# Perceiver block on one core: the context of the cross-attention is loaded in both layouts, and its layer norm moves into weights and probabilities

## What is computed

```python
    def _L0_xattn_ref(modality1, modality2, ln1_g, ln1_b, ln2_g, ln2_b, Wq, bq, Wk, bk, Wv, bv, Wo, bo):
        ...
        E = Wq.shape[1]
        scaling = E ** (-0.5)
        x1 = layernorm(modality1, ln1_g, ln1_b)
        x2 = layernorm(modality2, ln2_g, ln2_b)
        q = x1 @ Wq + bq
        k = x2 @ Wk + bk
        v = x2 @ Wv + bv
        scores = jnp.einsum('bqe,bke->bqk', q, k) * scaling
        attn = jax.nn.softmax(scores, axis=-1)
        ctx = jnp.einsum('bqk,bke->bqe', attn, v)
        return ctx @ Wo + bo
    ...
    x = x + _L0_xattn_ref(_layernorm(x, axis=-1), ctx_768, ...)
```

## Time and profile before

| | |
|---|---|
| median of 3 runs | 584.26 us (583.65 to 586.27) |
| the profiled execution, its own time | 584.41 us |
| its span | 582.5 us |
| TensorE busy | 504.2 us, 87% |
| VectorE busy | 390.8 us, 67% |
| ScalarE busy | 284.8 us, 49% |
| GpSimd busy | 115.6 us, 20% |
| moved by DMA | 98.74 MB, mean 170 GB/s |

### The profile page before, as it was taken

How to read it: one execution, slowest core, us unless ns; L and a number is a source line. 1 busy time by engine, 2 the same in 40 slices (tenths; PEclk the granted TensorE clock), 3 DMA queues, 4 the chain that set the end, 5 groups by cost and what they waited for, 6 DMA issues and landing times.

```text
span 582.5 us, 11091 instructions
## 1 busy us (share of the span) xinstructions
PE 504.2 (87%) x3601; PEld 294.1 (50%) x3602; DVE 390.8 (67%) x876; ACT 284.8 (49%) x449; POOL 115.6 (20%) x89
## 2 busy tenths in 40 slices
PE   5799999989989899976720699999999999999993
PEld 3674656474657577755420244444444444544441
DVE  2889779827987989889785666665563736673230
ACT  0662768685356666666610444463544525552130
POOL 1212113112323040400670002112111111121112
PEclk9899999999989999996755789999999999999998
DMA  9992606000006996162397358987584875744232
GB/s 323 390 383 101 218 1 217 2 1 2 1 0 249 379 382 239 38 217 77 128 307 252 55 179 254 258 262 221 126 244 117 231 218 159 235 80 87 54 54 37
DMA packets 54962, 98.74 MB, mean 170 GB/s; under 512 B 25073, under 2 KB 26257, under 8 KB 50833
## 3 DMA queue, kind: packets, MB, share of 16 engines
q1 hardware_dynamic: 23984, 74.81, 36.7%
q10 hardware_dynamic: 26640, 13.73, 9.8%
q0 software_dynamic: 4304, 9.77, 7.8%
HBM read 63.36 MB, written 29.43 MB: 159 GB/s over the span
## 4 chain that ended last, share of the span: by engine, by line
PE 69%; DVE 11%; ACT 6%; issue 5%; POOL 5%; DMA 3%; SPq 0%; ACTq 0%; POOLq 0%; DVEq 0%
PE bank L695 20%; PE bank L713 19%; PE bank L343 7%; PE bank L511 5%; POOL routed_rows L1637 3%; PE bank L495 2%; PE bank L425 2%; PE bank L455 2%; PE bank L361 2%; PE bank L405 2%; PE bank L537 2%; PE bank L476 1%; DMA routed_rows<-shared,ints 1%; ACT ctxT_region L741 1%; PE bank L588 1%
## 5 line engine op out<-in xcount | busy, mean ns | idle before, releaser
L695 PE MATMUL bank<-wbuf,ctx_region 128*128 x504 | 116.2, 388 | 6.3 <-issue 5.3
L1419 DVE SCALAR_TENSOR_TENSOR wbuf<-ctx_region,wbuf 128x2048 f32 (+1 forms) x28 | 62.9, 2289 | 31.9 <-ACT wbuf L880 31.9
L1667 POOL DMA_INDIRECT out<-misc,ints x21 | 38.6, 1839 | 229.7 <-ACT misc L961 174.5
L695 PEld LDWEIGHTS bank<-wbuf,ctx_region 128*128 128x128 f16 x504 | 49.0, 100 | 65.7 <-issue 13.5
L880 ACT ACTIVATE wbuf<-ctx_region 128x2048 f32 (+1 forms) x28 | 51.9, 1902 | 28.7 <-issue 22.5
L1569 POOL TENSOR_TENSOR small<-small 128x2 f32<-128x2 f32 (+2 forms) x25 | 29.5, 1182 | 173.8 <-DVE small L1034 167.2
L713 PE MATMUL bank<-wbuf,actT 128*128 x264 | 58.8, 379 | 1.0 <-DVE actT L1529 1.0
L980 ACT ACTIVATE ctxT_region<-bank 128x512 f32<-128x512 f32 x42 | 25.1, 597 | 67.9 <-PE bank L695 67.9
L713 PE MATMUL bank<-wbuf,xn 128*128 x240 | 53.4, 379 | 0.0
L511 PE MATMUL bank<-ctx_region,wbuf 128*128 128x256 f16 x384 | 44.9, 279 | 4.3 <-DVE ctx_region L1165 3.4
L511 PEld LDWEIGHTS bank<-ctx_region,wbuf 128*128 128x128 f16 x384 | 38.1, 100 | 11.2 <-DVE ctx_region L1165 4.1
(11 more groups left out here) (214 smaller groups left out, 820.0 us busy)
## 6 DMA issues: line engine op xcount, KB each, us to landing
ctx_region<-in_experts SPq DMA_DIRECT2D x28, 1024.0 KB
routed_rows<-ctxT_region SPq DMA_DIRECT2D x1, 16900.0 KB, 50.7
ctx_region<-in_ctx SPq DMA_DIRECT2D x8, 1536.0 KB, 8.9
ctx_region<-routed_rows ACTq DMA_DIRECT2D x23, 260.0 KB, 3.6
wbuf<-in_experts SPq DMA_DIRECT2D x4, 1024.0 KB
out<-x ACTq DMA_DIRECT2D x8, 256.0 KB
x<-in_x SPq DMA_DIRECT2D x1, 1536.0 KB, 14.3
wbuf<-in_wqT SPq DMA_DIRECT2D x4, 256.0 KB, 4.1
```

Of the source, the lines that this page charges most:

```text
L695: mm = nc.tensor.matmul(bank[half][:, :], xgT[:, b, x_part, k * P:(k + 1) * P], w16[:, ds(at + (w_part + k * EH + half * 512), 512)], star ...
L1419: nc.vector.scalar_tensor_tensor(w16[:, ds(at + (LOW + n * PIECE), PIECE)], src_[:, piece], W_SCALE, w16[:, ds(at + (HIGH + n * PIECE), PI ...
L1667: nc.gpsimd.indirect_dma_start(out, bass.IndirectOffsetOnAxis(idx[:, slot_no:slot_no + 1].bitcast(U32), axis=0), y_out[:, slot_no, :], Non ...
```

## The change

The context is no longer normalised. It is read raw, in two layouts: `ctx_768` as before from SyncE's queue, and a new input `ctxT`, the same numbers already turned on the host (left key included), 1.58 MB a tile, from ScalarE's queue straight into `ctxT_region`. The mean is taken out of the weights (`fold` subtracts from Wk's rows, already times the norm's gain, their mean over the channels; the sums over the context get their own mean subtracted by ScalarE), gain and shift of the norm go into Wk, the bias terms and `m2`. The inverse root of each key multiplies the scores and, after the softmax, the probabilities:

- TensorE: `context_T` and the turning of the left keys go; `roots_spread` comes, once a pair, with 16 products of 32x128 and 8 of 32x1 that lay each key's inverse root along a row for all 128 queries.
- ScalarE: `ctx_copies` and `ctx_norm` go; `load_ctxT` (two issues a pair, each behind the scores that free its slot), `roots_out` (2 copies of 257 columns), `queries_scaled` (2 of 128x512, before on VectorE), a sum, a small step and a second pass on each `cv` come; the copies of `pT` and `p_left` go to VectorE.
- VectorE: `ctx_scale`, `left_keys` and half of `sums_low` go; the scores' product with the spread roots, `probs_scaled`, `fold` and `value_bias` come; `ctx_stats` stays in full, and moves behind `probs_scaled`.
- SyncE: context tiles 6 and 7 are now followed by the self-attention's weights, which were early before.

```diff
             sp.dma_start(x_tiles[:, 0:2], x_dram[:, 0:2]).then_inc(s["x_in0"], 16)
+            sp.dma_start(ln2_rows, t_in["ln2_rows"]).then_inc(s["ln2_in"], 16)
...
-            for tile in range(4, TILES):
-                sp.wait_ge(s["cv_ps"], tile - 3)
-                load_ctx(tile)
+            for pair in range(1, PAIRS):
+                if pair + 1 < PAIRS:
+                    for t in range(2):
+                        sp.wait_ge(s["cv_ps"], 2 * pair - 1 + t)
+                        load_ctx(2 * pair + 2 + t)
+                if pair == 2:
+                    sp.wait_ge(s["qkb_ps"], 1)
+                    load_w(swq, "swqT", s["self_qk_in"])
+                    load_w(swk, "swkT", s["self_qk_in"])
+            load_w(swv, "swvT", s["self_vo_in"])
+            load_w(swo, "swoT", s["self_vo_in"])
...
             for e in range(KC):
-                if e % 2 == 0:
-                    pe.wait_ge(qk_in[e // 2], 64)
+                pe.wait_ge(qk_in[e], 32)
+                pe.wait_ge(s["folded"], e + 1)
...
+            def roots_spread(pair):
+
+                pe.wait_ge(s["x1T"], pair + 1)
+                pe.wait_ge(s["cx_rstd"], 2 * pair + 2)
+                if pair == 0:
+                    pe.wait_ge(s["left_rstd"], 1)
+                for t in range(2):
+                    tile = 2 * pair + t
+                    for b in range(BT):
+                        rows_of, at = slice(b * L, (b + 1) * L), dict(start=True, stop=True, tile_position=(0, b * L), skip_group_check=True)
+                        for c2 in range(2):
+                            nc.tensor.matmul(bank[t][rows_of, c2 * P:(c2 + 1) * P],
+                                             cx_rstd[:, tile % 4, 2 * b + c2:2 * b + c2 + 1].to_broadcast([P, L]), ident, **at)
+                        mm = nc.tensor.matmul(bank[t][rows_of, KEYS - 1:KEYS],
+                                              ident[0:B, tile * BT + b:tile * BT + b + 1].to_broadcast([B, L]), l_rstd[0:B, :], **at)
+                    mm.then_inc(s["r_ps"], 1)
...
                 for k in range(CC):
                     if k == 1:
                         pe.wait_ge(s["q_bias"], 1)
+                        roots_spread(0)
+                    if k == 2:
+                        pe.wait_ge(s["r_out"], 2)
...
-                    context_T(2 * pair + 2)
                     asked(pair + 1)
-                    context_T(2 * pair + 3)
+                    roots_spread(pair + 1)
                     sums_T(pair)
...
+            def load_ctxT(tile):
+                act.dma_start(ctxT[:, tile % 2].rearrange("p c b k -> p (c b k)"), t_in["ctxT"][tile]).then_inc(ctxT_in[tile % 2], 16)
...
+            queries_scaled(1)
+            roots_out(0)
             for pair in range(PAIRS):
...
+                    nc.scalar.activation(cv[:, t, :], bank[2 + t][:, 0:DC], ACT.Copy, scale=sc_rinv[:, t:t + 1],
+                                         accum_out=cv_sum[:, t:t + 1]).then_inc(s["cv_raw"], 1)
+                    act.wait_ge(s["cv_raw"], 2 * tile + 1)
+                    nc.scalar.activation(cv_shift[:, t:t + 1], cv_sum[:, t:t + 1], ACT.Copy, scale=-1.0 / DC).then_inc(s["cv_raw"], 1)
+                for t in range(2):
+                    act.wait_ge(s["cv_raw"], 4 * pair + 2 * t + 2)
+                    scaled(cv[:, t, :], cv[:, t, :], 1.0, cv_shift[:, t:t + 1]).then_inc(s["cv"], 1)
...
+            def fold(e):
+
+                dve.wait_ge(qk_in[e], 32)
+                key_w = wkT[:, e, 0:DC]
+                count(nc.vector.scalar_tensor_tensor(unread[:, 0:DC + 1], wkT[:, e, 0:DC + 1], 1.0, ln2_b_row[:, 0:DC + 1], ALU.mult,
+                                                     ALU.mult, accum_out=wkT[:, e, DC:DC + 1]), "norm_step")
+                count(nc.vector.scalar_tensor_tensor(key_w, key_w, 1.0, ln2_g_row, ALU.mult, ALU.mult,
+                                                     accum_out=wk_sum[:, e:e + 1]), "norm_step")
+                nc.vector.scalar_tensor_tensor(key_w, wk_sum[:, e:e + 1].to_broadcast([P, DC]), -1.0 / DC, key_w, ALU.mult,
+                                               ALU.add).then_inc(s["folded"], 1)
...
-                    count(nc.vector.tensor_reduce(sc_max[:, one], bank[2 + t][:, 0:KEYS], AX.X, ALU.max), "max_step")
+                    count(nc.vector.tensor_tensor(of_keys, bank[2 + t][:, 0:KEYS], spread[:, t, 0:KEYS], ALU.mult), "max_step")
+                    count(nc.vector.tensor_reduce(sc_max[:, one], of_keys, AX.X, ALU.max), "max_step")
...
+            def probs_scaled(pair):
+                for t in range(2):
...
+                    nc.vector.tensor_tensor(pT[:, t, :].rearrange("p (c b q) -> p c b q", c=2, b=BT),
+                                            bank[4 + t][:, 0:2 * P].rearrange("p (c b q) -> p c b q", c=2, b=BT),
+                                            cx_rstd[:, tile % 4, :].rearrange("p (b c) -> p c b", c=2)[:, :, :, None].to_broadcast(by_key),
+                                            ALU.mult).then_inc(s["pT"], 1)
```

More of the change, by code:

```diff
@@ L610, in logits @@
                     mm.then_inc(s["z_ps"], 1)
-            context_T(0)
-            pe.wait_ge(s["left_n"], 1)
-            transposes(bank[7][:, 320:416], [left_n[0:B, k * P:(k + 1) * P] for k in range(CC)], s["left_ps"])
             asked(0)
-            context_T(1)
             for pair in range(PAIRS):
@@ L851, in _ @@
+                    nc.scalar.copy(x2a[:, 0, :, t * P:(t + 1) * P], bank[4 + t][:, 0:DC].rearrange("p (k t) -> p k t", k=CC))\
+                        .then_inc(s["x2a_hi"], 1)
+                if pair + 2 < PAIRS:
+                    queries_scaled(pair + 2)
             cut_self_high(2)
@@ L1053, in ctx_stats @@
-            def ctx_stats(tile):
-                u, part = tile % 2, ctx_n[:, tile % 4]
-                if tile == 2 or tile % 2 and tile > 1:
-                    dve.wait_ge(s["cx_n1"], halved(tile - 2))
-                dve.wait_ge(ctx_in[tile % 4], 16 * (tile // 4 + 1))
-                pieces = [part[:, b, c2, :] for b in range(BT) for c2 in range(2)]
-                norm_stats(pieces, cx_stats[:, u], cx_mv[:, u], cx_ve[:, u], s["cx_ve"])
-            def ctx_scale(tile):
+            def ctx_stats(tile, parts=(0, 1)):
@@ L1071, in ctx_scale @@
-                for i, piece in enumerate(pieces[0:4] if half else pieces):
-                    op = normalise(piece, piece, cx_mv[:, u, i, 0:1], cx_rstd[:, u, i:i + 1])
-                op.then_inc(s["cx_n0"], 1)
+                if 0 in parts:
+                    if tile > 1:
+                        dve.wait_ge(s["cx_rstd"], tile - 1)
+                    dve.wait_ge(ctx_in[tile % 4], 16 * (tile // 4 + 1))
+                    for i in range(4):
+                        count(nc.vector.bn_stats(cx_stats[:, u, i, :], pieces[i]), "norm_step", wait=False)
@@ L1098, in queries_low @@
                 nc.vector.tensor_tensor(x1[:, 1], x1T, x1[:, 0], ALU.subtract).then_inc(s["x1_lo"], 1)
-            def left_keys(pair):
-                for t in range(2):
-                    tile = 2 * pair + t
-                    nc.vector.tensor_copy(ctxT[:, t, :, :, KEYS - 1], left_T[:, :, tile * BT:(tile + 1) * BT]).then_inc(s["left_cols"], 1)
             def context_max(pair):
```

336 lines of the change are left out of this document (158 added, 178 removed).

## The result

The changed kernel takes 590.28 us (median of 6 runs, 586.6 to 592.77) against 584.17 in the runs beside it: ratio 1.0099, 95% interval 1.0058 to 1.014. It is slower by about 6 us, where 4.7 us less were predicted. The profiled execution takes 591.1 us with a span of 588.8 (before 584.41 and 582.5). Executions of one kernel differ (the mean granted clock of the six of the change lies between 0.925 and 0.934), so a trace stands for one execution, and its time is given where it lies far from the median.

What follows compares the result with a forecast made beforehand. TensorE was taken as the bound (busy 87% of the span, 26.2 us a pair). Pairs -9.1, head +3.0 and tail +1.4 sum to -4.7, so 584.4 becomes 579.7 us (579.6 against the median); range 571 to 590.

Steps and rivals of the forecast that it cites:

- Removal of the turning: TensorE's context transposes and the waits on their copies go: 7.38 us a pair, 22.1 us in three pairs.
- The spread: New root products on TensorE, once a pair: 4.2 us taken, with ends of 1.5 and 6.9.
- the dear rival: Spread on TensorE at 6.9 us a pair, kernel slower than before at 590 us; chance 0.16.
- The head: Up to the first sums: scores 11 us early, but first sums at 62.3 instead of 59.31, 3.0 us more.
- The clock in the pairs: Three pairs: no term for lower clock, 2.5 us added only before the first sums; below 1.0 would contradict the prediction.
- The tail: After the last sums, extra passes on each cv: 1.4 us more before the self-attention.
- Behind the stage: After about 145 us no instruction changes; everything there is taken to move as a whole.
- VectorE's 21.2 us a pair: VectorE's work in a pair sums to 21.2 us, below TensorE's 23.0, with 1.8 us to spare.
- the transfers at nothing: Later context tiles and ctxT's issues on ScalarE are taken to cost no time; as a rival 586 us, chance 0.10.
- the prediction's own signs of being wrong: First sums after 66, clock below 1.0 in pairs, scores waiting for DMA, or a difference behind the self-attention's start.
- Rival (b): Spread dear: 6.9 us a pair, pairs 1.2 less, head 5.5 more, tail 1.4: +5.7, 590 us; chance 0.16.
- Rival (a): Spread cheap: four column tiles overlap, 1.5 us a pair, VectorE becomes the bound: 572.7 us; chance 0.20.

Runs made afterwards that it cites:

- e7_left_last: Changed kernel with the spread's one-column products moved behind the wide ones, whose order stays: 574.85 us, ratio 0.9822 to the kernel before.
- e2_wide_left: Changed kernel with the spread's order kept and its one-column products run over 128 rows: 580.12 us, ratio 0.9904 to the kernel before.
- e5_no_turned_loads: Changed kernel with turned context loaded only for tiles 0 and 1, later pairs' scores reading those: 588.86 us, ratio 1.0079 to the kernel before.
- e1_order: Changed kernel with the spread's loops exchanged (neighbours on different column tiles) and one-column products behind the wide ones: 574.74 us, ratio 0.9805 to the kernel before.
- e8_all: Changed kernel with loops exchanged, one-column products last on 128 rows, second join ahead of first spread, VectorE reordered in first pair: 573.23 us, ratio 0.9808.
- e12_last_wide: Changed kernel with one-column products last and on 128 rows, wide ones in the change's order: 574.52 us in a single execution.
- e6_no_spread: Changed kernel without a spread in pairs 1 to 3, which use the first pair's spread roots: 581.64 us, ratio 0.9939 to the kernel before.

## Why the prediction was wrong

The miss is 11.4 us in the profiled execution (579.7 against 591.1).

- **Removal of the turning, 22.1 us: right.** A pair of 26.2 - 7.4 + 5.6 = 24.4 stands against 24.55 measured.
- **The spread, 4.2 us: the step that failed.** It measured 5.6, which is 4.2 us in three pairs. Its two terms were wrong in opposite directions. "Alone" on a column tile was taken to cost 0.214 a wide product, 3.4 us in all; in that order without the changes of mode between them, 16 wide products take some 1.2 (e7_left_last: 0.60 for eight). The one-column products were taken at 0.1 each, with nothing for the change of row mode; each makes TensorE change its mode and back, and that costs 3.3 us a pair (e2_wide_left). The rule of the Trainium skill was at hand (TensorEngine Tiling (Array Packing), Key Properties): the prediction says that by it the time would be near 590. I gave that outcome 0.16, because "one-column work is small" and the nearest row showed only 0.2 us. Measured, it is 0.4 us for each one-column product, and only the dear rival had a term for it.
- **The head, +3.0: wrong by 4.4.** First scores and the first pause were right (29.17 for 28.5, 2.69 us for 2.5). What was missed: the dear spread at the lower clock (9.3 us, where the sum had 4.2 and 2.5 for the clock), and the bias rows behind tile 2's statistics. I had added these on VectorE alone and not asked which of them TensorE waits for twice. (The terms there add up to 59.6, not 59.8.)
- **The clock in the pairs: missed, 5 us.** The sum had the lower clock only in the head. Behind the pauses at 60 to 67 the granted clock is 0.50 far into the first pair (29.5 for 24.55). How much of this comes differs between executions: with the same spread and head, the first pair of e5_no_turned_loads lasts 26.7.
- **The tail, +1.4: right in size (1.2), partly by luck.** Only 0.7 lie where the sum had them, before `sums_T`; the other 0.6 come behind it. The terms named there do not give 1.4 either.
- **Behind the stage, nothing: wrong by 2.2,** in the other direction: 1.1 by a wait for VectorE that went, 1.5 by the clock, less 0.4 later. VectorE's work on the last output reaches past 145 and did change.
- **VectorE's 21.2 us a pair, not the bound: right** for the change, whose second and third pair have no wait on TensorE before their last sums; so were the transfers at nothing (e5_no_turned_loads).

The parts 4.4 + 9.0 - 0.2 - 2.2 give 11.0 of the 11.4 us; the other 0.4 is the time outside the span (2.3 us, before 1.9). The 9.0 are the spread's 4.2 and the clock's 5.0, less 0.2. Three of the prediction's own signs of being wrong came: first sums later than 66, a clock below 1.0 in a pair, and a difference behind the self-attention's start. Rival (b) named the outcome, 590, but the number came out by luck: its spread of 6.9 was 3.9 us too dear in three pairs and it had nothing for the gain behind the stage, while its head was 1.9 too short and the 5 us of clock in the first pair were missing. Rival (a), a spread of 1.5 us at 572.7, did not hold for this order; it is what e1_order built: 1.5 us and 574.7.

## What to carry to other kernels

In this kernel small products cost what they interrupt: group them on TensorE by the rows and columns of the array that they use, and count the changes of shape, not the columns. Where a change brings work forward, follow the late engine (here VectorE) through the whole head, since TensorE's pauses can return as lower clock in work that did not change. And ask after each cheapened step what is late next: here a context tile that long pairs had hidden.

## What the runs showed of the hardware

- Sixteen 128*32 weight loads take 0.40 us when they follow each other, four between changes of row mode 0.35; the loads stand still for 0.20 us before those of a 32*32 product (e7_left_last and the change).
- 24 small products on four column tiles take 1.10 us in turn (e8_all) and 1.25 with two neighbours on a tile (e12_last_wide); with a third neighbour, of one column, 2.3 (e2_wide_left); with that one on 32 rows, so with sixteen changes of row mode, 5.6 (the change).
- The same pause can be followed by either level of the clock. Behind 2.49 us, 48 products took 7.08 us in the kernel before (0.50 from 172 to 174 us) and 5.42 in the change; behind 1.25 us, they took 5.41 in the change and 7.08 in e6_no_spread. What in TensorE's earlier activity decides it was not tried.
